# A whitening, Fourier filter and MLP kernel: the MLP's first matmul from a split in two fp32r parts to plain fp32 on two row parts of the array, its second with stationary weights in two column parts

## What is computed

```python
# stage 0: whitening over all 50176 tokens
f = x_flat - m; ff = (1-EPS)*cov(f) + EPS*I
x = solve_triangular(cholesky(ff), I) @ f * gamma + beta
# stage 1
residual = x
h = layer_norm(x, n1_g, n1_b)
# filter, per frequency: two block-diagonal complex layers between rfft2 and irfft2
o1 = relu(complex_matmul(rfft2(h), w1) + b1)
o2 = softshrink(complex_matmul(o1, w2) + b2, 0.01)
h = irfft2(o2) + h + residual
residual = h
h = layer_norm(h, n2_g, n2_b)
h = gelu(h @ mw1 + mb1)          # 64 -> 256
h = h @ mw2 + mb2                # 256 -> 64
return h + residual
```

## Time and profile before

| what | value |
|---|---|
| median of 3 runs | 1024.01 us (1020.97 to 1026.23) |
| the profiled execution: its time | 1024.67 us |
| the profiled execution: its span | 1022.9 us |
| TensorE matmul busy | 899.1 us (88%) |
| TensorE weight load busy | 780.4 us (76%) |
| VectorE busy | 717.3 us (70%) |
| ScalarE busy | 505.4 us (49%) |
| GpSimd busy | 261.5 us (26%) |

### The profile page before, as it was taken

One profiled execution on the slowest core, in us unless ns is written; L12 is line 12 of the kernel. 1 busy time (PEld: TensorE's weight loads), 2 busy tenths in 40 slices (PEclk: granted clock), 3 DMA queues, 4 the chain that ended last, 5 costly groups with the idle time before them and its releaser, 6 DMA issues.

```text
span 1022.9 us, 18505 instructions
## 1 busy us (share of the span) xinstructions
PE 899.1 (88%) x6391; PEld 780.4 (76%) x6391; DVE 717.3 (70%) x2063; ACT 505.4 (49%) x947; POOL 261.5 (26%) x107
## 2 busy tenths in 40 slices
PE   5889972887999988998999899998999999799687
PEld 5886552785789768976997699878987997599465
DVE  4456779179967876787678767776778788743762
ACT  0002001563676565756575657555755655675333
POOL 2000001333433133213321342234223422430110
PEclk8995565897999999999899989999999999999799
DMA  9940102002000210011001200020000000000001
GB/s 253 264 114 18 46 1 63 1 1 63 1 20 19 61 31 18 18 41 50 18 19 33 58 9 27 18 73 9 27 19 11 20 19 29 1 28 22 16 28 37
DMA packets 9956, 40.97 MB, mean 40 GB/s; under 512 B 1232, under 2 KB 1232, under 8 KB 8208
## 3 DMA queue, kind: packets, MB, share of 16 engines
q1 hardware_dynamic: 9888, 40.19, 14.2%
HBM read 27.34 MB, written 12.85 MB: 39 GB/s over the span
## 4 chain that ended last, share of the span: by engine, by line
PE 55%; DVE 24%; issue 10%; DMA 5%; ACT 4%; DVEq 0%; SPq 0%; ACTq 0%
PE psum L1054 15%; PE psum L1039 8%; PE psum L992 8%; DMA n<-x_dram 5%; DVE stats L543 5%; PE psum L973 4%; PE psum L922 3%; PE psum L861 3%; PE psum L934 3%; PE psum L944 3%; PE psum L1013 3%; DVE o_g L294 2%; ACT o_g L1146 2%; PE psum L909 2%; DVE n L584 2%
## 5 line engine op out<-in xcount | busy, mean ns | idle before, releaser
L1178 ACT ACTIVATE hid<-psum,hbias 128x448 f32<-128x448 f32 x224 | 136.4, 634 | 151.4 <-PE psum L1039 150.5
L1054 PEld LDWEIGHTS psum<-prm,hid 128*112 128x112 f32 x1792 | 184.1, 180 | 8.5 <-ACT hid L1178 4.7
L1054 PE MATMUL psum<-prm,hid 128*112 128x96 f32 x1792 | 188.4, 264 | 2.2 <-ACT hid L1178 2.2
L364 POOL TENSOR_TENSOR hbuf<-hbuf,prm 112x1792 f32<-112x1792 f32 x15 | 51.6, 3440 | 333.8 <-DVE hbuf L617 333.8
L666 DVE TENSOR_TENSOR n2T<-psum,n2T 64x448 fp32r<-64x448 f32 x112 | 69.7, 622 | 89.0 <-ACT n2T L1170 87.6
L1039 PE MATMUL psum<-n2T,mw1h 128*128 128x448 f32 x224 | 103.4, 461 | 25.2 <-DVE n2T L666 11.9
L392 POOL TENSOR_TENSOR p_y<-over,under 116x512 f32<-116x512 f32 x64 | 77.6, 1214 | 158.1 <-ACT under L1196 158.1
L992 PE MATMUL psum<-cst,p_y 116*128 116x224 f32 (+1 forms) x480 | 100.6, 352 | 3.0 <-POOL p_y L392 3.0
L992 PEld LDWEIGHTS psum<-cst,p_y 116*128 116x128 f32 (+1 forms) x480 | 89.0, 191 | 5.9 <-POOL p_y L392 3.2
L1039 PE MATMUL psum<-n2T,mw1l 128*128 128x448 f32 x224 | 84.3, 376 | 0.0
L371 POOL TENSOR_TENSOR rbuf<-hbuf,ybuf 112x3584 f32<-112x3584 f32 x8 | 62.9, 7865 | 70.0 <-DVE fbuf L703 63.9
(11 more groups left out here) (114 smaller groups left out, 1662.4 us busy)
## 6 DMA issues: line engine op xcount, KB each, us to landing
xin<-x_dram SPq DMA_DIRECT2D x9, 1568.0 KB, 9.0
out_dram<-oslice SPq DMA_DIRECT2D x56, 224.0 KB, 2.2
ybuf<-x_dram SPq DMA_DIRECT2D x2, 1568.0 KB, 20.1
fbuf<-x_dram SPq DMA_DIRECT2D x2, 1568.0 KB, 23.5
n<-x_dram SPq DMA_DIRECT2D x2, 1568.0 KB, 26.6
xin<-x_dram SPq DMA_DIRECT2D x4, 392.0 KB, 6.2
prm<-params_dram SPq DMA_DIRECT2D x1, 899.5 KB, 28.7
cst<-consts_dram SPq DMA_DIRECT2D x1, 716.0 KB, 20.5
```

The costliest lines, as they stand in the source:

```text
L1054: last = nc.tensor.matmul(t[0:ROWS, at:at + 96], hid[:, m, w % 2, (w // 2) * ROWS:(w // 2 + 1) * ROWS], pp("mw2")[:, 128 * m + zeros:128 * ...
L1178: nc.scalar.activation(hid[:, q % 2, q // 2, :], ring_c[k % RING_C][:, 0:4 * ROWS], ACT.Gelu, bias=hbias[:, q % 2:q % 2 + 1]).then_inc(c_a ...
```

## The change

- The first matmul of the MLP is plain fp32. `n2T` is one [128, 448] tile without rests, copied by ScalarE in one instruction. For each m, v = 0 multiplies on rows 0 to 63 of the array, v = 1 on rows 64 to 127, each into a bank of its own. `ev_rest`, `mw1h` and `mw1l` are gone.
- In the second matmul `mw2` is stationary and the hidden values move, 448 columns: v = 0 writes partitions 0 to 63 of the bank, v = 1 partitions 64 to 127 (two column parts of the array). ScalarE adds `mb2` and evicts to `mlp_t` (`ev_mlp_t`), four transposes (`turn_out`) bring tokens back to the partitions, VectorE adds the residual. These run one slice later: `mlp_out(s-1)` and `turn_out(s-1)` stand inside slice s, and those of slice 6 between the `inv_h` at the step's end.
- The second layer norm doesn't subtract the mean. The mean is taken out of the weights once (`mwm_ps`, `mw1s`), and `ln2` keeps one multiplication for each half and two small steps fewer.
- Shrinkage is v - clamp(v, -0.01, 0.01): VectorE clamps right behind its eviction, GpSimd subtracts, ScalarE has no part. `bias_f` is gone.
- PSUM: 3 banks for the filter, 3 for the MLP (v = 0, v = 1, and one shared by `transpose_n`, `mlp_out` and `turn_out`). `layer_1` writes over six banks, those of the MLP too.

```diff
+B_BANK = [k % RING_B for k in range(B_CHUNKS)]
+B_BANK[L1:L1 + 8] = [1, 2, 3, 4, 0, 5, 1, 2]
+C_ORDER = [("n2", 0)]
+for _s in range(SLICES):
+    C_ORDER += [("hid", _s, m, v) for m in range(2) for v in range(2)]
+    if _s > 0:
+        C_ORDER.append(("mlp", _s - 1))
+    if _s < SLICES - 1:
+        C_ORDER.append(("n2", _s + 1))
+    if _s > 0:
+        C_ORDER.append(("out", _s - 1))
+C_BANK = [what[3] if what[0] == "hid" else 2 for what in C_ORDER]
...
@@ VectorE @@
                 def ln2(i):
                     mean_rstd(i, 1)
                     for k in range(2):
-                        subtract_mean(fbuf, n2, 1, k)
-                        multiply_rstd(n2, i, 1, k).then_inc(n2_ready, 1)
+                        multiply_rstd(i, k)
...
-                            dve.wait_ge(shrunk, i * 8 + c - L2_BUFS + 1)
+                            dve.wait_ge(y_ready, i * 8 + c - L2_BUFS + 1)
...
+                        nc.vector.tensor_scalar(clamped[:, c % L2_BUFS, 0:n], layer2[:, c % L2_BUFS, 0:n], LAM, -LAM,
+                                                ALU.min, ALU.max).then_inc(shrunk, 1)
...
-                def ev_rest(i, s):
...
@@ TensorE @@
+                def mlp_in(i, s, m):
+                    if m == 0:
+                        pe.wait_ge(c_act, i * C_ACT + C_ACT_DONE["n2", s])
+                    for v in range(2):
+                        t = free_c(i, C_AT["hid", s, m, v])
+                        nc.tensor.matmul(t[:, 0:4 * ROWS], mw1s[C * v:C * v + C, HH * m:HH * m + HH],
+                                         n2T[C * v:C * v + C, :], start=True, stop=True).then_inc(pe_c, 1)
+
+                def mlp_out(i, s):
+                    t = free_c(i, C_AT["mlp", s])
+                    pe.wait_ge(c_act, i * C_ACT + C_ACT_DONE["hid", s, 1, 1])
+                    for m in range(2):
+                        for v in range(2):
+                            last = nc.tensor.matmul(t[C * v:C * v + C, 0:4 * ROWS], pp("mw2")[:, C * m:C * m + C],
+                                                    hid[:, s % 2, m, v, :], start=(m == 0), stop=(m == 1))
+                    last.then_inc(pe_c, 1)
+
+                def turn_out(i, s):
+                    t = free_c(i, C_AT["out", s])
+                    pe.wait_ge(c_act, i * C_ACT + C_ACT_DONE["mlp", s])
+                    for w in range(SW // 2):
+                        last = nc.tensor.transpose(t[0:ROWS, w * 128:w * 128 + 128],
+                                                   mlp_t[:, w * ROWS:(w + 1) * ROWS], ident)
+                    last.then_inc(pe_c, 1)
+
                 def mlp(i, s, fill):
...
+                    mlp_in(i, s, 0)
+                    fill(0)
+                    fill(1)
+                    mlp_in(i, s, 1)
+                    if s > 0:
+                        mlp_out(i, s - 1)
                     fill(2)
                     if s < SLICES - 1:
                         transpose_n(i, s + 1)
                     fill(3)
+                    if s > 0:
+                        turn_out(i, s - 1)
...
                     if behind:
+                        pe.wait_ge(b_act, i * B_ACT + b_done("act", L2 - 1))
+                        pe.wait_ge(b_dve, i * B_DVE + b_done("dve", L2 - 1))
                         transpose_n(i - 1, 0)
...
@@ ScalarE @@
-                def shrink(i, c):
...
+                def ev_mlp_t(i, s):
+                    k = C_AT["mlp", s]
+                    act.wait_ge(pe_c, i * C_CHUNKS + k + 1)
+                    nc.scalar.activation(mlp_t[:], ring_c[C_BANK[k]][:, 0:4 * ROWS], ACT.Identity,
+                                         bias=pp("mb2")).then_inc(c_act, 1)
```

362 lines of the change are left out of this document (156 added, 206 removed).

## The result

The changed kernel has a median of 1028.61 us (1024.05 to 1039.55, 20 runs) against 1023.78 (1015.15 to 1031.50, 20 runs) for the kernel before beside it; ratio 1.0062, 95% interval 1.0041 to 1.0082. It is slower by 0.6%; forecast were 1005 us (972 to 1052) and a gain. The profiled execution took 1033.73 us, its span 1031.8.

What follows compares the result with a forecast made beforehand. TensorE was taken to bound the slices and VectorE's chain to count between pairs. 1024.7 - 25 (TensorE) + 14 (new waits) - 11 (between pairs) + 1.5 (pair 0) + 1 (tail) = 1005 us, range 972 to 1052.

Steps and rivals of the forecast that it cites:

- TensorE's sum: MLP matmuls in each slice: 4.36 us of TensorE against 4.87, -0.51; -25 us over 49 slices beside a filter.
- B: Rival: `mlp_in`'s row parts run staggered, by program order, only middle records overlapping; a pair costs 1.13 us; 1035 us; 17%.
- A: Rival: the second matmul's column parts don't overlap, so `mlp_out` takes 3.02 + 0.19 us; 1074 us; 18%.
- New waits in the slices: Waits from the MLP's shared bank, mainly in slices 5 and 6: +2 us a pair, +14 (0 to +35).
- C: Rival: VectorE falls behind in slices 1, 2 and 6, output eviction listed ahead of `layer_2`'s fourth; 1019 us; 10%.
- its mark of 5: Slices: the forecast counts as wrong if new waits take more than 5 us a pair.
- Between the pairs: Seven boundaries: later restart against shorter VectorE norm; -8 in four with a load, -1 each in three; -11 (-35 to 0).
- The reading that code comes behind the load: VectorE's 7.01 us stall at its loop's turn: the loop's code is fetched behind the load of x.
- D: Rival: VectorE's restart is free, four boundaries lose 5 to 6 us more, new waits halve; 975 us; 10%.
- Pair 0: VectorE's added clamps cost +1.5 us in pair 0, where no MLP runs beside.
- The tail: MLP alone after the last pair's filter: slices of 7.6 us against 7.04; +1 us in all (-5 to +10).
- Set-up: The weights' mean adds one small matmul and one operation, two others go: 0.

Runs made afterwards that it cites:

- `before_load_early`: The kernel before the change, with SyncE's load of x issued one step earlier, behind the store of slice 3: 999.60 us, ratio 0.9787.
- `clamp_alone`: The kernel before the change, with only the clamped shrinkage (VectorE clamps, GpSimd subtracts, no ScalarE ReLU): 1020.03 us, ratio 0.9985.
- `norm_early`: The changed kernel with the next pair's first layer norm moved earlier in VectorE's list, slices 3 to 5: 1014.65 us, ratio 0.9933.
- `five_fixes`: The changed kernel with earlier norm, earlier x load, seven tail MLP banks, and small reorderings of the mean's matmul, `transpose_n` and `mlp_out`: 980.27 us, ratio 0.9626.
- `lend_filter`: `five_fixes` with the two whitening banks lent to the filter in slices 5 and 6 and behind them: 973.18 us, ratio 0.9522.
- `v_outer`: The changed kernel with the second product's four matmuls reordered, both halves m of column part v = 0 first, then v = 1: 1027.17 us, ratio 1.0051.
- `three_banks`: The kernel before the change, with three filter banks in place of four and one bank left unused: 1049.21 us, ratio 1.0296.
- `lend_hid`: `five_fixes` with the two whitening banks lent to the second half of the hidden units in slices 4 to 6: 980.61 us, ratio 0.9593.
- the two early loads: The load of x issued one step earlier, in the changed kernel (1020.29 us, ratio 0.9996) and in the kernel before (999.60 us, ratio 0.9787).
- `mean_alone`: The kernel before the change, with only the second layer norm's mean folded into the weights: 999.50 us, ratio 0.9782.

## Why the prediction was wrong

The forecast for seven sets of slices was -25 us of TensorE and +14 of new waits, -11. Measured is +10.6. Where the pairs differ is read from TensorE's starts, in us, at a granted clock of 1.00 or close to it:

| | slice 0 | slices 1 to 4 | slice 5 | slice 6 to the next `dft_h` |
|---|---|---|---|---|
| `before_load_early` | 8.0 | 42.3 | 7.6 | 13.5 |
| `clamp_alone` | 8.0 | 41.4 | 7.6 | 13.5 |
| the changed kernel | 6.4 | 40.6 | 7.5 | 18.2 |
| `norm_early` | 6.4 | 40.6 | 7.5 | 16.7 |
| `five_fixes` | 5.6 | 41.0 | 7.5 | 15.3 |
| `lend_filter` | 5.9 | 41.0 | 7.5 | 14.4 |

Slices 1 to 4 of `clamp_alone` and of the changed kernel, and the last column of `before_load_early` and of the changed kernel:

```profile
394.68:436.09 41.41, 41.41 (x328) 40.44 (x326) 34.32 (x104) 20.98 (x39) 12.91 (x9) 1.00 0.07 23
502.16:542.74 40.58, 40.33 (x245) 28.10 (x245) 26.93 (x94) 21.63 (x39) 12.84 (x9) 1.00 0.05 17
```

```profile
536.43:549.97 13.54, 12.68 (x73) 8.87 (x72) 10.87 (x24) 6.07 (x13) 3.22 (x1) 1.00 0.11 34
550.23:568.47 18.24, 14.65 (x64) 6.47 (x63) 13.00 (x29) 7.40 (x15) 3.21 (x1) 1.00 0.08 26
```

The second matmul of slice 0 (3.1 us before) now runs in the last column, so the first and the last column belong together: 21.6 us became 24.6. Slices 1 to 5 are 1.8 us shorter. The whole loss is behind slice 5.

**TensorE's sum, right in what overlaps, half in size: one step that failed.** Row parts overlap though a wait stands between them (B is false), column parts overlap (A is false), and B's ground, program order, doesn't fit `v_outer`. But the sum has 4.36 us a slice against 4.87, -0.51, and slices 1 to 4, where TensorE hardly waits, give (41.41 - 40.58 + 0.25 of waits) / 4 = 0.27. The blocks themselves cost what was forecast or less (2 x 0.95, 1.66, 0.39). What the sum has too low are the changes of shape: in slice 1 the four pieces of `layer_2` take 0.1 to 0.2 more each and `turn_out` 0.2 more, so that with what is inside the blocks it comes to 1.3 us a slice where the sum has 0.95. (What went was a little dearer than the sum has it: only four of the eight fp32r matmuls stand back to back, and the eight took 1.88 us, not 1.8.) At 0.27 the term is -13 us in place of -25.

**New waits in the slices, the other step that failed.** "I take +2 us for each pair, 7 pairs: +14 (0 to +35)". With the clamp, which the sum put at nothing and which `clamp_alone` shows to save 0.8 us a pair, and 7 x 0.27 off, the slices at full clock would take 70.6 - 1.9 = 68.7 without new waits. They take 72.4 (slice 0 then takes 6.05), so the waits are 3.7 us a pair, +26 in place of +14. The runs name them: 1.6 VectorE's norm in the way of slice 6 (`norm_early`), 1.3 the place of `mlp_out` at the pair's end (16.7 to 15.3 in `five_fixes`), 0.9 the three filter banks that I "put at nothing" (`three_banks`, and `lend_filter` again). The earlier `transpose_n` of `five_fixes` only moved its wait: slice 0 is 0.45 shorter, slice 1 0.42 longer. I had looked for the waits of the MLP on itself; in slice 5, where I had them, they are 0.4 us (`lend_hid`). The larger ones were of the filter behind the MLP's evictions in VectorE's list. C named the right engine with the wrong place: the eviction ahead of `layer_2` does no harm, the one ahead of the norm in slice 3 does. By the text's own count, with 0.51 a slice off and the clock in it, the new waits come to 6.0 us a pair (73.3 against 70.9 less 3.6), above its mark of 5.

**The clock, left out.** The waits cost twice, since TensorE came out of some at half the rate. Against the same stretches at full clock that is 8.9 us over the six sets of the changed kernel and 4.9 in the kernel before. The sum had no term for it. With it the terms close: -13, +26, -6 for the clamp and +4 make +11.

**Between the pairs, right in sum.** Forecast -11, measured -11.2: -9.9 in the four with a load (forecast -8), -1.4 in the other three (-3). The restart is 3.0 us later against `dft_h` (2.2 forecast), but the statistics end only 0.6 later, and the two subtractions are gone. The reading that code comes behind the load is borne out by the two early loads and by the `instruction` packets. D, a free restart, did not come; that its time of 975 is about what the fixes reach by another way is chance.

**Pair 0.** Forecast +1.5, measured -0.2. The clamp alone costs 3.6 there; `mean_alone` has pair 0 2.1 us shorter, and the rest was not tested.

**The tail.** Slices of 7.47 us, forecast 7.6. It grew by 3.6 us where +1 was forecast: its first two slices ran at a granted clock of 0.59, against 1.00 in the next four. The kernel before too starts its tail low, but for 7.0 us (0.66 from 965.60 to 972.60, then 1.00), not for 16.8.

```profile
970.86:987.67 16.81, 13.47 (x36) 5.30 (x36) 2.91 (x24) 6.33 (x11) 0.00 (x0) 0.59 0.01 1
987.67:1017.62 29.95, 21.57 (x97) 8.70 (x96) 7.18 (x19) 13.93 (x24) 0.00 (x0) 1.00 0.10 31
```

**Set-up, forecast 0.** The mean's matmul stands on the path for 1.0 us. Of the other 5.1 of this execution 4.7 arise ahead of that matmul, and most is not shown to be part of the change: `dft_h` first starts at 186.2 us here, but between 179.1 and 184.8 in the six profiled runs that leave the changed set-up as it is, and between 178.1 and 180.7 in four with the set-up of before. It goes with the landing of x's first loads, the last of which is at 70.4 us here and at 66.6 in the kernel before.

```profile
79.92 1.08 PE L825 MATMUL psum<-mw1s,pilot_w 64*128 64x256 f32 x2
```

## What to carry to other kernels

A matmul made cheaper is worth only what the lists beside it let through: look, for each engine, at what stands in its list behind the operation that now waits, and at what that costs when the engine it feeds comes sooner. Test the parts of a large change alone; here one line's worth of algebra gave 2.2% and the rest took it back. Compare two kernels slice by slice, from start to start: a change can pay in most slices and lose it all in one place. When an engine stalls at its loop's turn, look for a large transfer that was issued just ahead, and move that first.
